# Twelve classes of 261 nodes, paired Exps and a deeper look-ahead in the attention scatter of a graph kernel

## What is computed

```
h = (x @ W_gat).reshape(M, HEADS, NUM_EXPERTS)            # 4 heads x 4
e = leaky_relu(a_src[src] + a_dst[dst], 0.2)
ee = exp(e - e_max[dst])
denom = segment_sum(ee, dst);  alpha = ee / denom[dst]
agg = segment_sum(h[src] * alpha, dst) + b_gat
scores = layernorm(agg).mean over heads;  top 2 of 4, softmax -> g
out = sum over experts of g * (gelu(x @ W1 + b1) @ W2 + b2)
```

## Time and profile before

| | us |
|---|---|
| median of 3 runs | 4361.2 |
| lowest, highest | 4360.7, 4361.96 |
| span of the profiled execution | 4602.8 |

### The profile page before, as it was taken

The page is one execution under the profiler, slowest core; times in us unless marked ns, Lnnn a source line. Parts: engine busy times, 40 slices in busy tenths (PEclk is TensorE's granted clock), DMA queues, the critical chain, the costliest instruction groups (busy, mean ns, idle before and its releaser), DMA issues. The chain is left out here.

```text
span 4602.8 us, 88005 instructions
## 1 busy us (share of the span) xinstructions
PE 3885.9 (84%) x23733; PEld 3489.0 (76%) x23733; DVE 2976.4 (65%) x7006; ACT 2107.0 (46%) x4811; POOL 2125.1 (46%) x2102
## 2 busy tenths in 40 slices
PE   7899999999999988989995666667666699999993
PEld 6798898989889877987885655556556578888883
DVE  7698898989889876554332222222321488989888
ACT  3565565656556536763221000000000288989882
POOL 0455555555555501000006666666666167667671
PEclk9899999999999987999995555665655599999996
DMA  4466666656556610004443333333333123323225
GB/s 138 135 176 171 171 175 171 177 170 175 169 170 177 169 31 23 24 26 161 151 150 103 89 87 89 92 87 91 87 89 90 52 55 75 63 67 70 60 48 120
DMA packets 226998, 509.09 MB, mean 111 GB/s; under 512 B 51805, under 2 KB 94299, under 8 KB 220426
## 3 DMA queue, kind: packets, MB, share of 16 engines
q0 software_dynamic: 116736, 313.66, 24.7%
q1 hardware_dynamic: 106389, 187.30, 14.6%
q10 hardware_dynamic: 3679, 5.79, 0.4%
HBM read 434.08 MB, written 72.49 MB: 110 GB/s over the span
## 5 line engine op out<-in xcount | busy, mean ns | idle before, releaser
L685 POOL DMA_INDIRECT big<-table,e_idx x784 | 751.2, 958 | 1049.6 <-DVE e_idx L721 649.0
L356 POOL DMA_INDIRECT big<-table,e_idx x784 | 767.0, 978 | 856.9 <-issue 304.1
L703 PE MATMUL psum<-e_near_hot,big 128*128 128x64 f32 x3136 | 621.9, 371 | 377.6 <-issue 361.9
L703 PEld LDWEIGHTS psum<-e_near_hot,big 128*128 128x128 f32 x3136 | 616.7, 292 | 391.7 <-issue 386.7
L2191 POOL DMA_INDIRECT g_S<-gsrc,g_idx x512 | 588.8, 1150 | 274.8 <-issue 157.8
L748 DVE TENSOR_TENSOR big<-big,psum 128x128 f32 x196 | 56.6, 289 | 801.9 <-remote 489.6
L435 ACT ACTIVATE e_hT_hi<-psum 128x256 fp32r<-128x256 f32 x784 | 300.2, 383 | 593.9 <-PE psum L375 513.1
L468 DVE TENSOR_TENSOR big<-psum,big 128x512 f32<-128x512 f32 x784 | 539.4, 688 | 45.5 <-issue 22.8
L386 PE MATMUL psum<-e_w_hi,e_hT_hi 128*128 128x256 f32 x1568 | 509.8, 325 | 0.3 <-issue 0.3
L386 PE MATMUL psum<-e_w_hi,e_hT_lo 128*128 128x256 f32 x1568 | 443.7, 283 | 0.0
L386 PE MATMUL psum<-e_w_lo,e_hT_hi 128*128 128x256 f32 x1568 | 440.7, 281 | 0.0
(11 more groups left out here) (397 smaller groups left out, 9090.5 us busy)
## 6 DMA issues: line engine op xcount, KB each, us to landing
big<-in_attr_t SPq DMA_DIRECT2D x392, 128.0 KB
g_rest<-gpart SPq DMA_DIRECT2D x128, 256.0 KB
big<-table,e_idx POOLq DMA_INDIRECT x1568
table<-C SPq DMA_DIRECT2D x26, 896.0 KB
table<-n_rows SPq DMA_DIRECT2D x24, 896.0 KB
experts<-g_region SPq DMA_DIRECT2D x15, 560.0 KB
g_S<-gsrc,g_idx POOLq DMA_INDIRECT x512
table<-big SPq DMA_DIRECT2D x25, 224.0 KB
```

Source lines behind the costliest of these rows:

```text
L356: pool.indirect_dma_start(G[:, j % 2, q, :], None, table, bass.IndirectOffsetOnAxis(idx[:, j, q:q + 1], 0)).then_inc(s[f"G_in{j % 2}{q}"], 16)
L685: pool.indirect_dma_start(G[:, j % n, q, :], None, c.table1, bass.IndirectOffsetOnAxis(idx[:, j, q:q + 1], 0)).then_inc(s[f"G_in{j % n}"], 16)
L703: last = pe.matmul(acc[:, b, :], G[:, j % n, q, b * 128:(b + 1) * 128], onehot[:, q, :], start=q == 0 and (b == 0 or s is sems[1]), stop=q ...
```

## The change

The diff does five things. `CLASSES, POS` becomes 12, 261, so the one-hot rows have 262 columns in place of 314, `spread` has 12 x 20 values for each part in place of 10 x 20, and a weight load has 120 columns in place of 100. All four tiles' one-hots are made on ACT; `last_hot` and its semaphore go. The Relu and the Exp of two steps are one instruction each, issued in every second ACT step, after the second of the two logits is there. DVE picks two steps ahead (it was one) and turns three ahead (two), PE looks up four ahead (three), SP loads five ahead (four). `scattered` itself now waits for `used`, as `last_hot` did, and one more turned and pick stand ahead of the loop.

```diff
@@ -38,7 +38,7 @@
 HUGE = 1e30
-CLASSES, POS = 10, 313
+CLASSES, POS = 12, 261
 WHOLE = 1.5 * 2.0 ** 23
@@ -2203,12 +2202,12 @@
                 act.wait_ge(s["hot_ready"], n)
-            for q in range(ON_ACT):
+            for q in range(SUP):
                 c.fence(act)
...
                                bias=pos[:, bass.ds(n * SUP + q, 1)]).then_inc(s["off_ready"], 1)
-            act.wait_ge(s["off_ready"], n * ON_ACT + ON_ACT)
-            act.activation(hot[:, j, 0:ON_ACT, :], off_row, ACT.Relu, scale=-1.0,
+            act.wait_ge(s["off_ready"], n * SUP + SUP)
+            act.activation(hot[:, j, :, :], off_row, ACT.Relu, scale=-1.0,
                            bias=c.ones[:, 0:1]).then_inc(s["hot_ready"], 1)
@@ -2535,13 +2534,6 @@
 
-            def last_hot(k, j):
-                n = k * ROW_SLOTS + j
-                dve.wait_ge(s["used"], n + 1)
-                c.fence(dve)
-                dve.tensor_scalar(hot[:, j % 2, SUP - 1, :], wide[:, :], pos[:, bass.ds(n * SUP + SUP - 1, 1)], None,
-                                  ALU.is_equal).then_inc(s["last_hot_ready"], 1)
-
             def classes(k, j):
@@ -2564,7 +2556,7 @@
                 n = k * ROW_SLOTS + j
-                dve.wait_ge(s["w_ready"], n + 1)
+                dve.wait_ge(s["w_ready"], k * (ROW_SLOTS // 2) + j // 2 + 1)
                 dve.tensor_tensor(R[:, j % 2, :, GH:CH].rearrange("p q (h e) -> p q h e", h=GH),
@@ -2573,6 +2565,7 @@
                 dve.wait_ge(s["class_ready"], n + 1)
+                dve.wait_ge(s["used"], n + 1)
                 dve.tensor_tensor(spread[:, j % 2, :, :, :], bc(at_class[:, j % 2, :, :], 3, CH),
@@ -2584,12 +2577,11 @@
                     indices(k + 1, j)
+                if ahead(3):
+                    turned(*ahead(3))
+                rest_of(k, j)
                 if ahead(2):
-                    turned(*ahead(2))
-                rest_of(k, j)
-                if ahead(1):
-                    pick(*ahead(1))
-                last_hot(k, j)
+                    pick(*ahead(2))
                 scattered(k, j)
@@ -2602,6 +2594,8 @@
             pick(0, 0)
+            turned(0, 2)
+            pick(0, 1)
             with dve.Fori(0, GSUP // ROW_SLOTS - 1) as k:
@@ -2673,8 +2667,8 @@
             def do_step(n, e, g, step):
-                if not (isinstance(n, int) and n + 4 >= GSUP):
-                    load_part(n + 4, (n if step is None else step) % 2)
+                if not (isinstance(n, int) and n + 5 >= GSUP):
+                    load_part(n + 5, 1 - (n if step is None else step) % 2)
                 if e is None:
@@ -2690,7 +2684,7 @@
 
-            for n in (2, 3):
+            for n in (2, 3, 4):
                 load_part(n, n % 2)
@@ -2734,7 +2728,6 @@
                 pe.wait_ge(s["hot_ready"], n + 1)
-                pe.wait_ge(s["last_hot_ready"], n + 1)
                 pe.wait_ge(s["spread_ready"], n + 1)
@@ -2746,8 +2739,8 @@
                         work[u][0](*work[u][1:])
-                    if u == 1 and not (isinstance(n, int) and n + 3 >= GSUP):
-                        look_up(n + 3, 1 - j)
+                    if u == 1 and not (isinstance(n, int) and n + 4 >= GSUP):
+                        look_up(n + 4, j)
 
@@ -2771,6 +2764,7 @@
             look_up(2, 0)
+            look_up(3, 1)
             program(pe, do_step)
@@ -2803,17 +2797,20 @@
 
-            def weights(n, j):
-                act.wait_ge(s["e_ready"], n + 1)
-                act.wait_ge(s["spread_ready"], n - 1) if not (isinstance(n, int) and n < 2) else None
-                act.activation(w[:, j, :, :], w[:, j, :, :], ACT.Relu, scale=-1.0).then_inc(s["below_zero"], 1)
-                act.wait_ge(s["below_zero"], n + 1)
-                act.activation(R[:, j, :, 0:GH], w[:, j, :, :], ACT.Exp, scale=-1.0).then_inc(s["w_ready"], 1)
+            def weights(n, pair):
+
+                both_w, both_R = w[:, :, :, :].rearrange("p j q h -> p (j q) h"), R[:, :, :, :].rearrange("p j q c -> p (j q) c")
+                act.wait_ge(s["e_ready"], n + 2)
+                if not (isinstance(n, int) and n == 0):
+                    act.wait_ge(s["halved"], 2 * n)
+                act.activation(both_w, both_w, ACT.Relu, scale=-1.0).then_inc(s["below_zero"], 1)
+                act.wait_ge(s["below_zero"], pair + 1)
+                act.activation(both_R[:, :, 0:GH], both_w, ACT.Exp, scale=-1.0).then_inc(s["w_ready"], 1)
 
...
                 j = (n if step is None else step) % 2
-                if not (isinstance(n, int) and n == GSUP - 1):
-                    weights(n + 1, 1 - j)
+                if j and not (isinstance(n, int) and n == GSUP - 1):
+                    weights(n + 1, (n + 1) // 2 if step is None else (e * NG + g) * (STEPS // 2) + (step + 1) // 2)
                 past = previous(n, e, g, step)
```

More of the change, by code:

```diff
@@ L2082, in stage_router_and_experts @@
     PW, PAD = POS + 1, TP
-    ON_ACT = SUP - 1
     assert CLASSES * POS >= NODES and CLASSES // 2 * CH <= 128
@@ L2125, in stage_router_and_experts @@
         taken = 3 * FB * GC + 3 * GROUP * D
-        off_row = region[:, taken:][:, 0:ON_ACT * PW].rearrange("p (q n) -> p q n", q=ON_ACT)
-        at_block = region[:, taken + ON_ACT * PW:][:, 0:ROW_SLOTS * SUP * NT].rearrange("p (j q t) -> p j q t", j=ROW_SLOTS, q=SUP)
-        assert 2 * NT * D >= taken + ON_ACT * PW + ROW_SLOTS * SUP * NT
+        off_row = region[:, taken:][:, 0:SUP * PW].rearrange("p (q n) -> p q n", q=SUP)
+        at_block = region[:, taken + SUP * PW:][:, 0:ROW_SLOTS * SUP * NT].rearrange("p (j q t) -> p j q t", j=ROW_SLOTS, q=SUP)
+        assert 2 * NT * D >= taken + SUP * PW + ROW_SLOTS * SUP * NT
         EARLY = (taken - NT * D) // D
@@ L2137, in stage_router_and_experts @@
         assert 2190 + ROW_SLOTS * SUP * CH <= 2 * GROUP * D
-        rest = sb("rest", [128, 8 * GSUP * SUP])
+        rest = sb("rest", [128, 6 * GSUP * SUP])
         cuts = [0]
@@ L2159, in stage_router_and_experts @@
         names = ("below_zero", "idx_ready", "begun", "cut", "part_in0", "part_in1", "turned_ready", "block_ready", "looked_up",
-                 "picked", "e_steps", "e_ready", "w_ready", "R_ready", "spread_ready", "off_ready", "hot_ready", "last_hot_ready",
+                 "picked", "e_steps", "e_ready", "w_ready", "R_ready", "spread_ready", "off_ready", "hot_ready",
                  "halved", "class_ready", "used", "own")
```

## The result

| | kernel before | changed kernel |
|---|---|---|
| median, us | 4361.6 (4360.7 to 4364.4, 4 runs) | 4336.5 (4334.1 to 4339.9, 4 runs) |
| ratio to before, 95% interval | | 0.9945 (0.9931 to 0.9959) |
| the same two once more, beside each other | 4361.8 (17 runs) | 4336.8 (5 runs), ratio 0.9943 (0.993 to 0.9956) |
| profiled span, us | 4358.7 (taken again) | 4338.1 |

The change is faster by 25 us. The forecast was 4320, so 41 us, with a range of 4300 to 4346: sign and range hold, the size is 16 us short. One more execution of the changed kernel in the second pair took 12967 us and is left out of its median and ratio. The question of this part is where those 16 us went.

What follows compares the result with a forecast made beforehand. ACT was taken to bound the step at 6.24 us, with PE and DVE within 5%; DVE at 5.90 would take over. 126 x (6.24 - 5.90) = 42.8, less 1.6 for the ends, gives 41 us: 4320 us, range 4300 to 4346.

Steps and rivals of the forecast that it cites:

- ACT's terms: ACT's step: paired Exps save 1.48 us, fourth one-hot adds 0.28, longer Relu 0.09; from 6.24 to 5.13 us.
- PE's spacing: Scatter matmuls on PE come 0.120 us apart instead of 0.142; PE needs at most 5.79 us a step.
- rival 1: PE becomes the bound because wider loads keep matmuls at 0.142 us; 4320 to 4350, middle 4335; chance 0.17.
- DVE's step: DVE becomes the bound: 5.95 less 0.30 and 0.10, plus 0.333 for the spread and 0.017 for classes, 5.90 us.
- The 0.10: Gap ahead of the removed comparison on DVE: 0.10 us a step goes too; without it the time is 4333.
- The 5.95: DVE's own step before the change, from one spread to the next where nothing holds it: 5.95 us.
- Stalls: 33 us of scattered stalls in the 128 steps stay as they are; bounds 15 us gained, 6 us given back.
- rival 3: Stalls of ACT and PE mostly vanish since DVE can't be held by them; 4295 to 4308; chance 0.15.
- The ends: Start of the stage +3.3 us, end -2.4 for two steps without pick, class borders +0.7; sum +1.6.
- Rival 2: GpSimd's gathers come late, without room to catch up; four open POOL stalls cost 10 us: 4330; chance 0.08.
- Rival 4: Nothing measurable, as all three engines and the ring between them make 6.24; within 8 us of 4361; chance 0.07.
- rival 5: DVE waits 2.5 us for the paired Exp ahead of weighted every second step, 158 us: 4478; chance 0.08.

Runs made afterwards that it cites:

- e3: Changed kernel with one Relu and one Exp for each step again; 4600.8 us, ratio 1.0043 to the kernel before, which took 4581.2 beside it.
- e1: Changed kernel with 10 classes of 313 positions again, block mask in a tile of its own; 4345.1 us, ratio 0.9965 to the kernel before.
- e2: Changed kernel with the fourth one-hot compared on DVE again, after pick, and no wait for used in scattered; 4366.3 us, ratio 1.0015 to the kernel before.
- e4: Changed kernel with the spread's three waits moved ahead of pick's long reduction, behind the wait for the multiply; 4345.2 us, ratio 0.9968 to the kernel before.
- e10: Changed kernel with three more, already met waits ahead of the spread; 4354.9 us, ratio 0.9986 to the kernel before.
- e0: The kernel before the change, unedited, profiled again; 4360.5 us in one run, profiled span 4358.7.
- e8: The changed kernel, unedited, measured again beside the kernel before; 4336.8 us, ratio 0.9943.
- e11: Changed kernel with scattered's waits and the gathered rows' wait between pick's multiply and reduce, two semaphores merged to save one wait; 4333.4 us, ratio 0.9934 to kernel before.
- e5: Changed kernel without two of the four gathers of every step from the fifth on; 4524.9 us, ratio 0.9878 to the kernel before, which took 4581.2 beside it.

## Why the prediction was right in sign and too large

**ACT's terms held.** Square 507 ns for a forecast 509, four in 1.73 us, Relu 1171 (forecast 1170), half the table loads. ACT is busy for 66.0 of 77.8 us, which is 5.14 a step of 6.06; forecast 5.13. e3 confirms the 1.48 of the pairing from the other side.

**PE's spacing held, rival 1 fell.** Eight loads of 120 columns now take 1.02 us:

```profile
4008.75 1.02 PEld L2735 LDWEIGHTS psum<-g_hot,g_spread 128*120 128x120 f32 x8
```

(1.02 - 0.19) / 7 = 0.119 us apart, forecast 0.120, before 0.142. PE as a whole is busy for 75.12 of 77.80 us, 5.85 a step, where at most 5.79 was forecast. e1 shows what rival 1 would have looked like, since there the 0.142 stay.

**DVE's step is the term that was mis-sized: 5.90 forecast, 6.055 measured.** Of its four parts three held: the comparison went (e2: worth 0.27, of 262 columns), the spread is 2.16, `classes` 0.25. Two errors make the 0.155.
- The 0.10 that I let go with `last_hot` didn't go. The reason given was that `scattered` has no register to compute. But it took over the wait for `used`, so that it has three waits on values of a register, and e4 and e10 show that such waits are what holds it: 0.09 with none, 0.19 with three, 0.36 with six. Worth 0.10 x 126 = 12.6 us. The end "DVE without the 0.10 gives 4333" was on record, and the result lies 3.5 us from it.
- The 5.95 on which the sum was built was the shorter of two kinds of step. In the earlier trace rows line 2532 follows line 2528 after 1.02; in the kernel before, profiled again, it is 1.02 or 1.13, 1.07 in the mean. That is another 0.055 a step, 7 us. One step can't show this; the mean over the stretch does. Two more gaps of that step were off and happen to cancel: 0.09 behind line 2511, where the changed kernel has 0.16 in the mean, and 0.57 behind line 2215, where it has 0.49. The step that the 5.95 came from, more of the earlier trace rows:

```profile
4411.06 0.16 DVE L2511 COPY g_idx<-g_src_i 128x4 int32 x1
4411.16 0.65 DVE L2215 TENSOR_SCALAR g_turned_hot<-g_rest,row 125x512 fp32r<-125x512 f32 x1
4411.73 0.24 DVE L2218 TENSOR_TENSOR g_region<-iota,g_rest 128x100 f32<-128x100 f32 x1
...
4413.07 0.99 DVE L2528 TENSOR_REDUCE g_picked<-g_chosen_rows 128x32 f32<-128x800 f32 x1
```

Together 0.155 x 126 = 19.5 us, more than the 16 missed.

**Stalls.** I left them as they were, with 15 us to gain and 6 to lose. The 33 us of the first profile were mostly of its execution (e0). Of the 14.3 that an execution of 4360 has, 10.4 went: rival 3 in part. At the first of the two places a step of 8.59 and one of 9.30 us in the kernel before became one of 7.95. DVE's wait for the Exp shrank there from 2.3 to 1.8 us, and its wait of 3.2 us for the look-up is gone. Look-ups one step further ahead would do that, and so would ACT and PE with slack, which is the reason rival 3 gave; no run tells the two apart.

**The ends.** Forecast +1.6, measured +8.1. At the start DVE stands 6.70 us for the look-up of step 2:

```profile
3486.34 0.99 DVE L2524 TENSOR_TENSOR g_chosen_rows<-psum,g_region 128x800 f32<-128x800 f32 x1 [6.70 <-PE psum L2754]
```

and the first spreads come 5.8 later instead of 3.3, which had been reckoned against a second spread that was itself late in that execution. Part of it is a cost that the forecast didn't have. ACT's first Exp now waits 1.1 us for the second of its two logits, PE stands idle 3.43 us for ACT's Gelu behind it, and PE's clock is then granted at the lower level, 1.2 GHz; in the kernel before PE stands idle 2.15 us at the same place and keeps 2.4 GHz. First the changed kernel, then the kernel before profiled again, eight expert matmuls and the stretch up to the end of the look-up behind them:

```profile
3480.18 4.53 PE L2197 MATMUL psum<-CT,g_w 128*128 128x312 f32 x8 [3.43 <-ACT g_region L2788]
3480.18:3486.30 6.12, 6.12 (x16) 4.44 (x16) 0.00 (x0) 2.43 (x6) 4.60 (x6) 0.52 0.30 51
3475.40 2.37 PE L2198 MATMUL psum<-CT,g_w 128*128 128x312 f32 x8 [2.15 <-ACT g_region L2794]
3475.40:3478.64 3.24, 3.24 (x16) 2.49 (x16) 3.00 (x7) 1.70 (x5) 2.56 (x3) 1.00 0.56 90
```

The granted clock is 0.52 in place of 1.00, and the same 16 matmuls take 6.12 us in place of 3.24: 2.9 of the 5.8 us. e1, e2, e4 and e8 to e11 show it too: PE idle for 3.0 to 3.7 us, then 3.9 to 4.5 us for the eight. At the end the two picks saved, 2.4 us, were met by the 4.9 us of waits for gathered rows (3.5 in the second profile): +3.0 for -2.4.

**Rival 2** happened in this small form, 4.9 of the 10 us it gave, and at the end only. Its floor of 5.75 us a step was not reached by the steady steps, and was by the last ones. The Trainium skill, in GPSIMD Engine Reference, Key points, has GpSimd contend with DVE instructions that have two SBUF inputs; the trace agrees (a gather of 0.94 takes 1.95 to 2.06 beside the spread). e5 prices the other direction: DVE's line 2214 holds its queue for 0.09 us less without a gather beside it.

**Rival 4** fell with the interval, **rival 5** with the 5.1 us of waits for the Exp. The 1.4 us of slack computed for its ring were enough while DVE is the bound; e1, with PE as the bound, shows the ring open.

So the account of the 16 us that are missing: 19.5 by DVE's step and 6.5 by the ends, less 10.4 that the stalls gave more than forecast; that is 15.6. That the range held is in part luck: the two terms that were too small would alone have given 4346, its upper end, and the stalls, left at nothing for want of a cause, made up for 10 us of it.

## What to carry to other kernels

When an engine becomes the bound, the gaps between its instructions are terms of the sum like the instructions: take them from the mean over the whole stretch, since a single step may be the shorter of two kinds, and count the waits ahead of each instruction, met or not (here 0.055 us for each after the first, on DVE, in a loop, where no long operation runs ahead of them). An operation taken from an engine hands its waits to the next one, so what disappears is its length and not the gap. And price a part of a bundle in its company: moving the one-hot without pairing the Exps, and the reverse, gained nothing here beside the twelve classes; all of it together gained 25 us. At the start of a stage, where PE still waits for others, look at its granted clock too: 1.3 us more of idle time came with 2.9 us of slower matmuls.

## What the runs showed of the hardware that was not expected

- A wait of DVE on a semaphore that is already met, with a value that is computed from the loop's register, costs: the spread starts 0.09, 0.19 and 0.36 us after the operation ahead with none, three and six of them; the same three with constants leave 0.11. Three behind a wait that is open cost 0.19. Ahead of it, under a running operation of 0.98 us, three and four of them cost alike, 0.07 to 0.10.
- The Trainium skill, in Perfetto Trace Analysis, Identifying Dependency Chains, says that an instruction that waits on several engines may have separate semaphore instructions put ahead of it. The numbers above would fit that; no trace here shows these instructions.
- The rows of a gather can be there long after its instruction has ended: the last one ended at 4245.50, and the sum that waits for rows started at 4254.22, 8.7 us later.
- A switch of ACT's table takes 1.28 us, and the next operation starts 1.29 to 1.30 after the load's start (3903.30, 3904.59). The Trainium skill, in ScalarE: Activation LUTs, What ACT_TABLE_LOAD costs, gives about 2.66 us for every switch, with a drain of 1380 ns beside the load of 1283. The load agrees, the drain is in no row here, and the measurement decides. An estimate from that page's figure, (2 x 2.66 + 0.40) / 2 = 2.86 us a step for the pairing, is nearly twice the 1.48 that e3 bears out.
- One and the same kernel took 4359 to 4362 us in three sets of runs and 4581 in one. The cause isn't shown by the traces.
